# Window attention on one core: the bias of V moved to ScalarE, V evacuated in front of the even part, and the per-image statistics re-cut into pieces that all stand in front of the reciprocal

## The reference, cut to what matters

```python
xs  = roll(group_norm(x, 32 groups), (-3, -3))
qkv = einsum('bchw,oc->bohw', xs, w_qkv) + b_qkv
# 7x7 windows, 8 heads of 16 channels
scores = einsum('...qd,...kd->...qk', q, k) / 4
out = einsum('...qk,...kd->...qd', softmax(scores), v)
x + roll(out, (3, 3))
```

## Time and profile before

| | us |
|---|---|
| median of 3 runs | 943.32 |
| lowest, highest | 942.41, 944.63 |
| the profiled execution, its own time | 941.08 |
| its span, first to last instruction | 938.9 |
| PE busy in the span | 865.0 |
| VectorE busy | 766.3 |
| GpSimd busy | 739.3 |
| ScalarE busy | 665.1 |

### The profile page before, as it was taken

The page is one execution under the profiler, slowest core; times in us unless marked ns, Lnnn a source line. Parts: engine busy times, 40 slices in busy tenths (PEclk is TensorE's granted clock), DMA queues, the critical chain, the costliest instruction groups (busy, mean ns, idle before and its releaser), DMA issues. The chain is left out here.

```text
span 938.9 us, 104445 instructions
## 1 busy us (share of the span) xinstructions
PE 865.0 (92%) x46473; PEld 708.7 (75%) x46473; DVE 766.3 (82%) x1399; ACT 665.1 (71%) x1297; POOL 739.3 (79%) x1191
## 2 busy tenths in 40 slices
PE   0479999998999999999999999999899999999994
PEld 0358888887788888887788888887678888888883
DVE  8657888889889888888888888888987777777873
ACT  2347777776677777777677777777677777777772
POOL 1347888887788888888788888888788888888883
PEclk9999999999999999999999999999999999999998
DMA  9401122112112211221211000000000000000001
GB/s 380 177 5 58 46 68 68 60 42 69 48 55 68 69 43 60 68 68 34 69 54 50 35 34 34 17 34 34 17 34 35 19 32 34 34 22 29 34 34 36
DMA packets 29912, 51.87 MB, mean 55 GB/s; under 512 B 3649, under 2 KB 28865, under 8 KB 29761
## 3 DMA queue, kind: packets, MB, share of 16 engines
q1 hardware_dynamic: 29888, 51.59, 15.8%
HBM read 25.89 MB, written 25.69 MB: 55 GB/s over the span
## 5 line engine op out<-in xcount | busy, mean ns | idle before, releaser
L373 ACT ACTIVATE probs_t<-psum,exp_scale 128x800 f32<-128x800 f32 x256 | 223.2, 923 | 139.6 <-PE psum L772 139.6
L571 DVE TENSOR_REDUCE neg_max<-psum 100x16 f32<-100x784 f32 x256 | 249.2, 974 | 39.1 <-PE psum L740 31.1
L291 POOL TENSOR_SCALAR mixed<-mixed,bias 128x392 f32<-128x392 f32 x128 | 161.7, 1263 | 123.2 <-DVE mixed L597 123.2
L740 PEld LDWEIGHTS psum<-k_hi,q_masks 32*128 32x128 f16 x8192 | 175.3, 91 | 46.3 <-issue 42.8
L740 PE MATMUL psum<-k_hi,q_masks 32*128 32x49 f16 x8192 | 197.8, 179 | 3.0 <-DVE neg_max L571 2.3
L740 PE MATMUL psum<-k_lo,q_masks 32*128 32x49 f16 x4096 | 182.6, 179 | 0.0
L740 PEld LDWEIGHTS psum<-k_lo,q_masks 32*128 32x128 f16 x4096 | 161.0, 91 | 0.0
L300 POOL TENSOR_TENSOR stage<-mixed,image 128x343 f32 (+7 forms) x256 | 144.2, 583 | 0.4 <-POOL mixed L291 0.4
L765 PE MATMUL psum<-q_masks,k_hi 32*64 32x100 f16 x8192 | 128.7, 219 | 16.1 <-DVE summed L588 13.3
L349 ACT ACTIVATE xn<-image,shift_c,rstd_c 128x21 f32 (+6 forms) x256 | 132.4, 573 | 8.0 <-DVE shift_c L551 6.1
L797 PE MATMUL psum<-probs_t,v_rows 64*32 64x100 f32 x8192 | 131.4, 252 | 2.4 <-issue 2.4
(11 more groups left out here) (112 smaller groups left out, 1828.2 us busy)
## 6 DMA issues: line engine op xcount, KB each, us to landing
out_dram<-stage SPq DMA_DIRECT2D x64, 224.0 KB, 2.1
out_dram<-stage SPq DMA_DIRECT2D x64, 168.0 KB, 1.9
image<-in_x_dram SPq DMA_DIRECT2D x32, 224.0 KB, 2.6
image<-in_x_dram SPq DMA_DIRECT2D x1, 6104.0 KB, 28.2
image<-in_x_dram SPq DMA_DIRECT2D x34, 168.0 KB, 2.5
image<-in_x_dram SPq DMA_DIRECT2D x6, 896.0 KB, 9.2
image<-in_x_dram SPq DMA_DIRECT2D x1, 728.0 KB, 14.3
w_nat<-in_L_conv_w_qkv_dram SPq DMA_DIRECT2D x1, 192.0 KB, 2.4
```

The source lines that it names most:

```text
L291: nc.gpsimd.tensor_scalar(mixed[:, half, :, :], mixed[:, half, :, :], bias[:, 2:3], None, ALU.add).then_inc(bias_added, 1)
L373: nc.scalar.activation(probs_t[:, 2 * u:2 * u + 2, :, :].rearrange("p h a q -> p h (a q)"), psum[:, COL_BANKS[u], 0:PAIRS * ROWS2], ACT.Ex ...
L571: nc.vector.tensor_reduce(neg_max[:, par, 2 * j:2 * j + 2, :], psum[0:ROWS2, ROW_BANKS, 0:GT] .rearrange("p h (w k) -> p h w k", k=TOK), A ...
L740: last = nc.tensor.matmul(psum[:, ROW_BANKS.start + h - 2 * j, w * TOK:(w + 1) * TOK], q_masks[rows, par, low + w * ROWS2:low + w * ROWS2 ...
```

## The change

On POOL `add_bias` goes away; on ACT it appears as an activation over the same tile, between `normalise` and `high_inverse`. `evac_v` and `evac_even` change places. On DVE the `between` places are gone: `change_image` now covers eight steps, and one piece of the chain stands in each, in front of the reciprocal. `change_image(1)` to `(3)` still end in the same step. The doubled steps of statistics become four for each of the images 2 and 3, and steps 2 and 3 of the start take a chunk each.

```diff
 # POOL
-            def add_bias(g, half):
-                pool.wait_ge(mixed_done, g + 2)
-                pool.sem_inc(waited, 1)
-                nc.gpsimd.tensor_scalar(mixed[:, half, :, :], mixed[:, half, :, :], bias[:, 2:3], None, ALU.add).then_inc(bias_added, 1)
...
             def step(g, n, par):
-                if live(g - 3):
-                    add_bias(g - 3, 1 - par)
                 if live(g - 1):
                     split_max(g - 1, 1 - par)
 # ACT
+            def add_bias(g, half):
+                act.wait_ge(mixed_done, g + 2)
+                nc.scalar.activation(mixed[:, half, :, :], mixed[:, half, :, :], ACT.Identity, bias=bias[:, 2:3]).then_inc(bias_added, 1)
...
                 if live(g + 2):
                     normalise(g + 2, n + 1, par, b)
+                if live(g - 3):
+                    add_bias(g - 3, 1 - par)
                 if live(g - 2):
                     high_inverse(g - 2)
+                if live(g):
+                    evac_v(g, par)
                 if live(g - 2):
                     evac_even(g - 2)
-                if live(g):
-                    evac_v(g, par)
...
-            for g in range(GROUPS - 2, GROUPS + 2):
+            for g in range(GROUPS - 2, GROUPS + 3):
                 step(g, g // 2, g & 1)
 # DVE
                 link(nc.vector.tensor_tensor(work_b[:, :], work_a[:, :], work_a[:, :], ALU.mult))
+                link(nc.vector.tensor_tensor(work_a[:, :], work_b[:, :], var_row[:, :], ALU.add))

             def group_variance():
-                link(nc.vector.tensor_tensor(work_a[:, :], work_b[:, :], var_row[:, :], ALU.add))
...
+            def norm_steps(b):
+                return [lambda: gather_channels(b), turn_channels, group_mean, group_variance] + NEWTON * [refine_root] + [lambda: offer(b)]
...
             def change_image(b):
-                g = (b * BANDS - 4) * 2
-                for ahead, between in ((None, lambda: gather_channels(b)),
-                                       (turn_channels, group_mean),
-                                       (group_variance, guess_root),
-                                       (lambda: refine_root(1), lambda: refine_root(1)),
-                                       (lambda: refine_root(NEWTON - 2), scatter_groups),
-                                       (None, lambda: offer(b))):
-                    step(g, g // 2, g & 1, ahead=ahead, between=between)
-                    g += 1
+                first = (b * BANDS - 5) * 2
+                for g, piece in enumerate(norm_steps(b), first):
+                    step(g, g // 2, g & 1, ahead=piece)
...
-            step(2, 1, 0)
-            step(3, 1, 1)
-            with dve.Fori(2, BANDS - 4) as n:
-                two_steps(n, 2 * n + 4, BANDS * BAND)
+            step(2, 1, 0, (8,), BANDS * BAND)
+            step(3, 1, 1, (9,), BANDS * BAND)
+            with dve.Fori(2, BANDS - 5) as n:
+                two_steps(n, 2 * n + 6, BANDS * BAND)
```

More of the change, by code:

```diff
@@ L521, in group_mean, with refine_root, offer @@
                 link(nc.vector.tensor_tensor(work_b[:, :], work_a[:, :], work_a[:, :], ALU.mult))
+                link(nc.vector.tensor_tensor(work_a[:, :], work_b[:, :], var_row[:, :], ALU.add))
             def group_variance():
-                link(nc.vector.tensor_tensor(work_a[:, :], work_b[:, :], var_row[:, :], ALU.add))
                 link(nc.vector.tensor_reduce(g_var[:, :], grouped(work_a), AX.X, ALU.add))
                 link(nc.vector.tensor_scalar(g_var[:, :], g_var[:, :], 1.0 / PER, EPS, ALU.mult, ALU.add))
-            def guess_root():
                 link(nc.vector.tensor_scalar(half_bits[:, :], g_var[:, :].bitcast(i32), 1, None, ALU.logical_shift_right))
                 link(nc.vector.tensor_scalar(rs[:, :].bitcast(i32), half_bits[:, :], -1.0, float(0x5F3759DF), ALU.mult, ALU.add))
[L534 to L541, removed]
+            def refine_root():
+                link(nc.vector.tensor_tensor(rs_t[:, :], rs[:, :], rs[:, :], ALU.mult))
+                link(nc.vector.scalar_tensor_tensor(rs_t[:, :], rs_t[:, :], -0.5, g_var[:, :], ALU.mult, ALU.mult))
+                link(nc.vector.scalar_tensor_tensor(rs[:, :], rs_t[:, :], 1.5, rs[:, :], ALU.add, ALU.mult))
+            def offer(b):
+                wait(dve, xn_ready, (b - 1) * 2 * BANDS)
                 nc.vector.tensor_scalar(grouped(mean_row), g_sum[:, :, None].broadcast_to([C, 8, PER]), 1.0 / PER, None, ALU.mult)
                 link(nc.vector.tensor_scalar(grouped(var_row), rs[:, :, None].broadcast_to([C, 8, PER]), X_SCALE, None, ALU.mult))
-            def offer(b):
-                wait(dve, xn_ready, (b - 1) * 2 * BANDS)
                 nc.vector.transpose(mean_c[:, :], mean_row[:, :])
@@ L599, in scale_rows, with step @@
                                         summed[:, :, :].rearrange("p (s a) q -> p s a q", s=2), ALU.mult).then_inc(mixed_done, 1)
-            def step(g, n, par, chunks=(), image_at=None, ahead=None, between=None):
+            def step(g, n, par, chunks=(), image_at=None, ahead=None):
                 if live(g):
@@ L612, in step @@
                     low_inverse(g - 2)
-                if between:
-                    between()
                 if live(g - 2):
@@ L650, in _ @@
                     take_stats(chunk * STAT, chunk)
[L651 to L658, removed]
+            for piece in norm_steps(0):
+                piece()
             work_out_scales()
@@ L671, in _ @@
                 first = b * BANDS - 1
-                for n in range(3):
+                for n in range(2):
                     dve.wait_ge(loaded[b + 1], 32 * -(-(2 * n + 2) * STAT // BAND))
@@ L675, in _ @@
                 dve.wait_ge(loaded[b + 1], 32 * BANDS)
[L676 to L680, removed]
+                for n in (2, 3):
+                    for par in range(2):
+                        chunk = 4 * (n - 1) + 2 * par
+                        step(2 * (first + n) + par, first + n, par, (chunk, chunk + 1), at)
+                with dve.Fori(4, CHUNKS // 2 - 2) as n:
+                    two_steps(n + first, 2 * n + 4, at)
             change_image(B - 1)
```

## The result

The changed kernel takes 996.36 us (median of 4 runs, 995.47 to 997.59) against 943.39 of the kernel before (4 runs): a ratio of 1.0562, with a 95% interval of 1.0543 to 1.058. The forecast was 969, with 957 to 983 as its range: the direction was right, the size was half of what came, and the time lies outside the range.

A forecast was written before the change was run, and what follows sets the result against it. The prediction took PE, gapless at 6.69 us per step, as the bound, with ScalarE's loop 0.17 us behind. Terms 38.3 - 12.0 - 0.6 = +25.7 on the 943.3 median gave 969, range 957 to 983.

The forecast's parts named there:

- the end: Kernel's end: the last bias costs 1.26 us on GpSimd and some 0.65 on ScalarE, so -0.6.
- What bounds the kernel: Normal step: PE runs without a gap at 6.69 us; the loop through ScalarE's even part has 0.17 us of slack.
- Part 1, the bias: ScalarE's queue: the bias activation takes 0.48 to 0.65 us, taken as 0.52.
- Part 2, odd step: Odd steps: bias and V in front of the even part shift the join 0.71; less slack, 0.54 each, +32.9.
- Part 2, even step: Even steps: bias hidden, V starts 0.14 behind the inverse, even part 0.26 later; less slack, 0.09 each, +5.4.
- Part 3, the pieces: Image changes on DVE: pieces in front of the reciprocal mostly fit the room; 5.0 us replaces 17.0, -12.0.
- A (faster): Normal step: ScalarE's extra work runs inside the slack, the period stays 6.69, time 931; 7%.
- B: Image changes: pieces meet GpSimd instructions or push the reciprocal, so 17.0 stays near 13, time 977; 12%.
- C: Even steps: `low_inverse` meeting GpSimd holds the join by 0.3, 18 us more, time 987; 8%.
- D, the PE clock: PE in normal steps: the new 0.54 gaps lower its granted clock, 49 us more, time 1018; 2%.

The follow-up runs named there:

- late_doubles: The changed kernel with the wait for all 16 bands of the next image back at its old place and the four doubled steps behind it; 975.56 us, ratio 1.0362.
- swap_unread: swap_only with PE's weighting reading a tile of weights in place of V, and V's evacuation not waiting for that weighting; 952.3 us, ratio 1.0086.
- swap_only: The kernel before with only the exchange: V evacuated in front of the even part, bias still on GpSimd, image change as it was; 980.06 us, ratio 1.0409.
- pieces_only: The kernel before with only the image change in eight pieces in front of the reciprocal and the late doubled steps; 933.98 us, ratio 0.9915.
- old_order: The changed kernel with the wait for the load at its old place and the even part in front of V again; 933.21 us, ratio 0.9914.
- gap_later_wait: bias_in_gap with the wait for all bands and the four doubled steps two steps later; 925.93 us, ratio 0.9832 against the kernel before.
- early_wait: The kernel before with only VectorE's wait for the last band of the next image moved two steps earlier; 960.29 us, ratio 1.0199.
- bias_in_gap: old_order with the bias in front of the exponentials, where ScalarE was idle, and GpSimd's add of the image one step later; 936.5 us, ratio 0.9947.
- swap_four: swap_only with four V buffers, V's wait two groups further back, and ScalarE's and PE's loops taking four steps per turn; 1625.13 us, ratio 1.7237.

## Why the prediction was right or wrong

The span grew by 55.3 us (938.9 to 994.2). By the prediction's steps:

| step | forecast | measured |
|---|---|---|
| odd steps: 61 forecast, 60 in the stretch measured | +32.9 (0.54 each) | +28.2 (0.47 each) |
| even steps: 60 forecast, 61 measured | +5.4 (0.09 each) | +22.6 (0.37 each) |
| image changes and doubled steps, 17.0 before | -12.0 | -16.4 (0.6 left) |
| stop of VectorE for the load of band 15, twice | not seen | +21.5 |
| the end | -0.6 | -0.4 |
| sum | +25.7 | +55.5 |

The measured terms are differences of rows: periods of the changed kernel less 6.69, 0.6 less 17.0 from late_doubles, and 882.4 less 860.9 for the stop. The stretch also begins 0.2 earlier, which makes the 55.3.

**What bounds the kernel: right.** The loop of exponentials, even part, join and column scores with 0.17 of slack is what was hit. In 84:967 of the changed kernel PE waits for the join in front of the column scores 121 times, 43.1 us in all, and swap_unread follows the loop's arithmetic to 0.01.

**Part 1, the bias: right.** 0.52 was forecast and 0.52 is measured; its length is 0.61 to 0.63. The estimate of 0.51 by the Trainium skill (ScalarE: Activation LUTs, "What ACT_TABLE_LOAD costs"), named in the prediction, was as good.

**Part 2, odd step: right in kind, 0.07 too high.** The step counted the three normalise pieces to the inverse as 1.25 of the queue, which they take in the kernel before (407.31 to 408.56); with a bias behind them they take 1.20 (417.82 to 419.02), and V follows the inverse by 0.12 and not 0.14. The rest was not tracked down.

**Part 2, even step: wrong.** The failed step is "V then starts at 402.08". The prediction took ScalarE's queue as the only thing that V waits for. `evac_v` has a second wait, for the weighting of two groups before, since V has two buffers. In the old order it never showed: the even part in front of V waits for that same weighting. PE's weighting ends at about +3.75, V starts at +3.84, the even part at +4.32 and not +3.79, 0.53 later; less the slack of 0.17 that is 0.36. In odd steps the bias fills the time until then, so the wait hides. swap_only (+38, forecast at +40 by this reading and +7 by the prediction's) and swap_unread show it.

**Part 3, the pieces: right, undersold.** The room in front of the reciprocal was there, and the time lost by the changes fell from 17.0 to 0.6 and not to 5.0. By my reading the reason is the loss itself: with the even part 0.4 to 0.5 late in every step, a late reciprocal is covered in even steps too. In a kernel whose steps stay near 6.69 the same pieces leave 10.0 (pieces_only, bias on GpSimd), 2.9 (old_order) or 3.8 (gap_later_wait). The forecast 5.0 lies between. Its guess that GpSimd without the bias gives the pieces more room is borne out in the masks of Q: by the fifth part of the pages, the 256 of them take 120.6 us before (L564) and 97.2 after (L559), 0.94 and 0.76 per step. The 10.0 against 2.9 and 3.8 fits it too, but neither pair is clean: old_order's odd steps are 0.14 longer, and gap_later_wait moves the add of the image as well.

**What part 3 left out: the stop.** This is the second failed step: the prediction counted the doubled steps' chunks by their length and never asked what the first of them waits for, so the term stood at nothing. The diff of late_doubles, read backwards, shows it: one round less in the loop over `n`, so the wait for all 16 bands comes two steps earlier. A step that is moved takes its waits along. early_wait prices it at 19 by the medians with nothing else changed.

**The rivals.** A (faster) was far off. B did not happen in the changed kernel (0.6 left, late_doubles); its mechanism, pieces that meet GpSimd, is seen in pieces_only, where 10.0 is left. C named the even step and came near its size (0.3 for a measured 0.28 more than forecast), but by another mechanism: `low_inverse` did not hold the join. D, the PE clock, did not show in normal steps: in 84:284 every 4 us stretch is at 1.00. Behind the stop it did, as the last section says. The range of 957 to 983 was missed because the even step was 17.2 too low and the stop, 21.5, was not in it. That the miss is no larger is luck: the odd steps were put 4.7 too high, and the changes saved 4.4 more than forecast.

## What to carry to other kernels

When two instructions of one queue are exchanged, read every wait of the one that moves forward: a wait that never showed may have been covered by the instruction now behind it, and a buffer's reader is as good a reason as its writer. When work is moved to an earlier step, ask when the data of its wait is issued, and wait only for what the step reads. Idle time of an engine is worth what stands behind it in the loop: the same bias cost 0.14 in every odd step in front of the inverse, and nothing in the gap in front of the exponentials.

## What the runs showed of the hardware that was not expected

**Behind a stop PE runs at half its clock for a while.** Windows of 4 us around the stop in the changed kernel: busy by engine, PE clock, DMA share, GB/s.

```profile
288.00:292.00 4.00, 0.55 (x3) 0.10 (x1) 0.00 (x0) 0.00 (x0) 2.77 (x6) 0.85 0.27 100
292.00:296.00 4.00, 1.00 (x48) 1.01 (x48) 1.83 (x5) 0.00 (x0) 0.00 (x0) 0.50 0.32 100
296.00:300.00 4.00, 2.26 (x133) 1.95 (x127) 2.93 (x6) 1.82 (x5) 0.00 (x0) 0.50 0.00 0
300.00:304.00 4.00, 4.00 (x102) 3.19 (x94) 2.94 (x6) 3.43 (x7) 1.45 (x4) 0.50 0.00 0
304.00:308.00 4.00, 3.70 (x211) 2.95 (x202) 2.15 (x4) 2.63 (x7) 3.15 (x4) 0.95 0.00 0
```

PE's first instruction behind the stop:

```profile
295.00 0.22 PE L722 MATMUL psum<-k_hi,q_masks 32*128 32x49 f16 x2 [6.44 <-DVE q_masks L559]
```

PE stood still for 6.4 us. Its granted clock fell to 0.50 (1.2 GHz) and was still there until about 304, while it worked again. In 300:304 it was busy throughout at 0.50, which by an estimate (4.00 x 0.50) is 2.0 us of work at the full clock; the step behind the stop took 9.24, 2.1 over a normal 7.16, and the pair lost 10.7 for a wait of 8.42. The clock is my reading of that rest. No run separates it from the time that the engines need to get back into step.

In bias_in_gap VectorE waited for only 2.14. PE's gaps there were 0.94 and 2.05, and the granted clock still fell, to 0.66 in 292:296 and 0.50 in 296:300. The pair of periods lost 5.1. In the changed kernel's normal steps, with gaps of 0.30 and 0.41, it stayed at 1.00.

**A kernel with a longer loop body ran far slower.** swap_four has four of PE's steps in the loop's body and not two, with the same instructions in all, and takes 1625 us: 6.75 MB of instruction loads in place of 0.18, and a mean PE clock of 0.757. That the length of PE's loop body is the cause is a reading; no run tried another length.
